# Two first tiles' products inside the routing chain of chunk 0, weight splits spread over its tiles, and the first coefficients loaded tile by tile

## The chip, the cores and the metric

The kernel runs on one core of a Trainium2 chip. The metric is the device time of one execution in microseconds (us); the time of the kernel before is the median of 3 runs. A profile is one execution recorded by the hardware profiler.

## The reference

Two layers run over 8192 tokens of 128 features (32 sequences of 256). Layer 0 adds to x a linear attention and a mixture of 64 experts with one shared expert, both on the normalized rows; layer 1 adds a windowed message network, a sparse top-8 attention and a mixture of 8 experts with 2 chosen. What the change touches is the expert part of layer 0:

```
xn = layernorm(x)
scores = sigmoid(xn @ router_w.T);  sfc = scores + e_bias
keep the 4 best of 8 groups (sum of a group's two largest), then the 8 best experts
coef[t, e] = 2.5 * scores / sum of the chosen, 0 elsewhere
h = silu(xn @ Wg[e]) * (xn @ Wu[e]) * coef[:, e];   out = sum over e of h @ Wd[e]  (+ shared expert)
```

## The kernel before

The tokens go in 16 chunks of 512. Features lie on partitions for the products. In layer 0 two experts of 64 hidden features make one tile of 128, so that a chunk has 33 tiles: 32 of experts and the shared one. All engines follow one plan of steps: step g is tile g of the whole run (chunk g // 33), and each engine does its part of the tile and then the side steps that the tables (`ATTENTION0`, `ROUTE0`, and so on) put at this tile. A list `PROLOGUE` is worked through before step 0.

**A tile.** TensorE (PE) computes at step g the gate and up products of tile g (`first_products`, `mm3`: three products of 128x512, since weights and rows are each split into a high part in a short format and a rest), and then the down product of tile g - 3 (`last_products`, L658). ScalarE (ACT) takes the silu of the gate bank (L1264), VectorE (DVE) multiplies with the up bank (`times_up`, L856) and, one step later, with the tile's coefficients (`times_coef`, L850). There are two gate banks, two up banks, one bank for the down products of a chunk and three side banks for all else. On every engine instructions run in the order written, so a wait holds all that stands behind it. The gate product of tile g waits for the silu of g - 2, the up product for `times_up` of g - 2, and `times_up` of tile g stands on DVE behind `times_coef` of g - 1.

**Coefficients.** DVE computes them for all 64 experts of a chunk in a chain of small operations (steps `sigmoid0` to `weigh`, L887 to L963), PE transposes them (`coefT`, L708), ACT copies them to SBUF (L1334), and the SP queue writes them to DRAM (`keep_coef`, L468). From there SP loads them with a broadcast over 64 partitions: a load (`load_coef`, L477) is two DMAs of 512 KB for the 4 tiles of one place in a ring of 3; a chunk has 8 loads.

**Weights.** In chunk 0 the gate and up weights of every tile are loaded raw by SP (`load_weights`, L417, 128 KB, 10 places) and split: a "split" step is a cast on ACT (L1292) and a subtraction on GpSimd (POOL, L1436), both kept in SBUF. There are 33 such splits, then 16 for the expert weights of layer 1 (L1297, L1439), whose result goes through 2 buffers to DRAM (`w_kept`, L502, 256 KB each): the ACT cast of part k waits until the DMA of part k - 2 has landed. Before, all 33 splits of layer 0 stand in the prologue, 24 of them ahead of the coefficients' transposes, and the 16 others at tiles 1, 3, ..., 31.

**The SP queue** issues all loads in one order. It goes through the splits n = 0, 1, ...: it waits for the POOL part of split n, issues raw weights n + 10, then what `load_rest` puts at n, and for layer 1 the DMA of `w_kept`. The first coefficients stand behind the 24th split, and the second chunk's `keep_coef` behind the last, which is in tile 31.

## Time and profile before

| | |
|---|---|
| median of 3 runs | 1779.98 us (1777.85 to 1780.35) |
| the profiled execution, its own time | 1780.57 us |
| its span | 1778.6 us |
| PE busy | 1713.6 us, 96% of the span |
| DVE, ACT, POOL busy | 1360.6, 806.6, 611.4 us |
| DMA moved | 269.80 MB, 152 GB/s on average |
| PE share of the chain that ended last | 93% |

The page gives busy times per engine and a chain of waits; the trace gives the instructions in order of time (start, duration, engine and line, the idle time before and what ended it), the busy time of each engine in any stretch, and for a DMA the time from issue to landing. Durations of PE are modelled, so the distance between the starts of two products is the better measure. Times below count from the start of the span.

### The profile page before, as it was taken

Reading aid. Unit: us, or ns where it says so; the run is one execution under the profiler, and the core shown is the slowest. Engines: PE = TensorE matmul, PEld = TensorE weight load, DVE = VectorE, ACT = ScalarE, POOL = GpSimd, SP = SyncE. Lnnn points to the kernel's source line nnn. Section 1 sums busy time; section 2 is a strip of 40 time slices with the busy share of each in tenths; the row PEclk is TensorE's granted clock in tenths of the full one; section 3 lists DMA queues with packets and bytes.
Section 4 is the critical chain, followed back from the end, with each engine's and each line's share of the span. In section 5 each row is a group of like instructions: output and inputs, shape, how many; then the busy total and the mean of one; then the engine's idle time right before and its main releaser. Section 6 shows DMA issues by size and latency. Waiting matters only on the chain.

```text
span 1778.6 us, 25081 instructions
## 1 busy us (share of the span) xinstructions
PE 1713.6 (96%) x7292; PEld 1216.1 (68%) x7292; DVE 1360.6 (77%) x4012; ACT 806.6 (45%) x1439; POOL 611.4 (34%) x656
## 2 busy tenths in 40 slices
PE   3999999999999999999999999999999998999995
PEld 2666777777777777777777777777777775667763
DVE  5667879796969797978787887878787877566557
ACT  4435454545444454545454535453545343554431
POOL 6212132323232323232323232232324143467770
PEclk9999999999999999999999999999999999999998
DMA  7948363736373636363736354554545445577759
GB/s 214 257 121 241 88 171 86 177 82 181 78 175 76 179 84 180 82 183 82 181 85 171 94 152 113 136 129 112 151 93 152 105 97 159 178 235 226 266 187 308
DMA packets 166470, 269.80 MB, mean 152 GB/s; under 512 B 13688, under 2 KB 52344, under 8 KB 166080
## 3 DMA queue, kind: packets, MB, share of 16 engines
q1 hardware_dynamic: 157760, 250.50, 52.8%
q0 software_dynamic: 8576, 17.70, 3.1%
q8 instruction: 61, 1.00, 0.2%
q14 instruction: 73, 0.60, 0.1%
HBM read 202.21 MB, written 65.93 MB: 151 GB/s over the span
## 4 chain that ended last, share of the span: by engine, by line
PE 93%; DVE 2%; DMA 1%; POOL 1%; issue 1%; ACT 1%; SPq 0%; DVEq 0%; POOLq 0%; ACTq 0%
PE ps_y L658 25%; PE ps_up L603 8%; PE ps_gate L605 8%; PE ps_up L605 8%; PE ps_gate L603 8%; PE ps_up L604 8%; PE ps_gate L604 8%; PE ps_y L684 4%; PE ps_side L624 3%; PE ps_side L605 2%; PE ps_side L603 2%; PE ps_side L604 2%; PE ps_side L793 1%; PE ps_side L776 1%; PE ps_side L735 1%
## 5 line engine op out<-in xcount | busy, mean ns | idle before, releaser
L856 DVE TENSOR_TENSOR silu_h<-ps_up,silu_h 128x512 f32<-128x512 f32 x618 | 423.6, 685 | 339.7 <-ACT silu_h L1264 271.1
L1264 ACT ACTIVATE silu_h<-ps_gate 128x512 f32<-128x512 f32 x618 | 368.1, 599 | 553.4 <-PE ps_gate L605 551.1
L658 PE MATMUL ps_y<-silu_h,w_dn 128*128 128x512 f32 x1056 | 540.7, 593 | 0.4 <-ACT yT L1270 0.4
L850 DVE TENSOR_TENSOR silu_h<-coef_b,silu_h 128x512 f32<-128x512 f32 x528 | 386.2, 731 | 12.0 <-DMA coef_b<-coef_kept 9.6
L603 PE MATMUL ps_gate<-xnT,w_gu 128*128 128x512 f32 x528 | 318.6, 603 | 0.2 <-ACT silu_h L1264 0.2
L658 PEld LDWEIGHTS ps_y<-silu_h,w_dn 128*128 128x128 f32 x1056 | 199.1, 189 | 54.7 <-issue 7.7
L603 PE MATMUL ps_up<-xnT,w_gu 128*128 128x512 f32 x528 | 209.4, 397 | 13.2 <-DVE silu_h L856 13.2
L605 PE MATMUL ps_gate<-xnT,w_gu 128*128 128x512 f32 x528 | 209.4, 397 | 0.0
L605 PE MATMUL ps_up<-xnT,w_gu 128*128 128x512 f32 x528 | 209.3, 396 | 0.0
L604 PE MATMUL ps_up<-xnT,w_gu 128*128 128x512 f32 x528 | 209.2, 396 | 0.0
L604 PE MATMUL ps_gate<-xnT,w_gu 128*128 128x512 f32 x528 | 208.0, 394 | 0.0
L1514 POOL DMA_INDIRECT slots_x<-rows,slot_of x120 | 133.8, 1115 | 178.2 <-PE ps_gate L605 152.6
L1520 POOL TENSOR_TENSOR msg<-msg 128x512 f32<-128x512 f32 x48 | 65.7, 1368 | 312.3 <-ACT msg L1400 309.8
L1493 POOL DMA_INDIRECT y_kept<-ys,y_to x148 | 145.3, 982 | 59.7 <-issue 38.3
L603 PEld LDWEIGHTS ps_gate<-xnT,w_gu 128*128 128x128 f32 x528 | 100.1, 190 | 60.9 <-issue 56.2
L604 PEld LDWEIGHTS ps_gate<-xnT,w_gu 128*128 128x128 f32 x528 | 100.4, 190 | 60.1 <-issue 55.8
L603 PEld LDWEIGHTS ps_up<-xnT,w_gu 128*128 128x128 f32 x528 | 99.5, 188 | 37.8 <-DVE silu_h L856 15.0
L604 PEld LDWEIGHTS ps_up<-xnT,w_gu 128*128 128x128 f32 x528 | 99.4, 188 | 24.0
L605 PEld LDWEIGHTS ps_up<-xnT,w_gu 128*128 128x128 f32 x528 | 99.4, 188 | 23.7
L605 PEld LDWEIGHTS ps_gate<-xnT,w_gu 128*128 128x128 f32 x528 | 99.5, 188 | 22.9
L1445 POOL TENSOR_TENSOR rstd<-rstd,minus_half 128x4 f32<-128x4 f32 x32 | 43.5, 1360 | 162.2 <-DVE shift L868 162.2
L684 PE MATMUL ps_y<-silu_h,w_down 128*128 128x512 f32 x180 | 91.6, 592 | 0.8 <-DVE silu_h L850 0.8
(266 smaller groups left out, 2699.3 us busy)
## 6 DMA issues: line engine op xcount, KB each, us to landing
coef_b<-coef_kept SPq DMA_DIRECT2D x256, 512.0 KB, 6.7
slots_x<-empty SPq DMA_DIRECT2D x15, 2080.0 KB, 12.2
w_block<-w_kept SPq DMA_DIRECT2D x45, 512.0 KB, 3.9
xs<-slots_x SPq DMA_DIRECT2D x37, 260.0 KB, 3.7
y_back<-y_kept SPq DMA_DIRECT2D x15, 512.0 KB, 6.0
w_raw<-in_ffn_w SPq DMA_DIRECT2D x49, 128.0 KB, 3.9
w_down<-in_ffn_w SPq DMA_DIRECT2D x45, 128.0 KB, 3.7
xres<-in_x SPq DMA_DIRECT2D x16, 256.0 KB, 3.2
```

Source lines behind the costliest of these rows:

```text
L603: eng.matmul(dst, w[0], m[0], start=start, stop=False)
L604: eng.matmul(dst, w[1], m[0], start=False, stop=False)
L605: return eng.matmul(dst, w[0], m[1], start=False, stop=stop)
L624: ins = eng.transpose(ps[:, r * P:(r + 1) * P], rows[:, r * P:(r + 1) * P], ident)
L658: eng.matmul(ps_y[:, :], w_dn[:, j], silu_h[:, g % HBUFS], start=j == 0, stop=last).then_inc(pe_down)
L684: eng.matmul(ps_y[:, :], w_down[:, t % BUFS1, f], silu_h[:, g % HBUFS], start=first, stop=last).then_inc(pe_down)
L850: eng.tensor_tensor(silu_h[:, s], coef_b[:, q % COEF_RING, k], silu_h[:, s], ALU.mult).then_inc(dve_h)
L856: eng.tensor_tensor(silu_h[:, s], ps_up[g % 2][:, :], silu_h[:, s], ALU.mult).then_inc(dve_h1)
L1264: eng.activation(silu_h[:, s], ps_gate[g % 2][:, :], ACT.Silu).then_inc(act_silu)
L1493: eng.indirect_dma_start(y_kept, bass.IndirectOffsetOnAxis(y_to[:, c % XPLACES, r:r + 1], 0), ys[:, c % BUFS1, r], None).then_inc(landed[c ...
L1514: eng.indirect_dma_start(slots_x, bass.IndirectOffsetOnAxis(slot_of[:, r, k:k + 1], 0), rows1[:, c % 2, r], None).then_inc(sent[c % 2], 16)
L1520: eng.tensor_tensor(msg[:, 0], msg[:, 0], msg[:, 1 + k % 2], ALU.add).then_inc(pool_heard)
```

## The change

The prologue keeps 10 splits. The others follow at the end of each tile of chunk 0: one of layer 0 a tile (tile g splits the weights of tile g + 10, up to tile 22), and one of layer 1 in every even tile, the last in tile 30. `SPLIT_ORDER` gives the order in which raw weights are loaded and split. The products, silus and up multiplications of tiles 0 and 1 are steps of the prologue ("gate0", "gate1", "up0", "up1"): the products stand before the transposes of the coefficients, the up multiplications behind them. The key and value products of the first two row blocks move ahead of these transposes as well; `q_sin`, `q_min` and the attention steps move 4 tiles or so back. SP keeps the first coefficients behind the sixth split, and loads the first 4 tiles' coefficients tile by tile (8 DMAs of 128 KB, with semaphores of their own). The constants, the second chunk's rows and the down weights are loaded at earlier places of the SP queue. POOL's fill of the last column of `empty`, which waits for the `common` constants, stands behind the first layer norm's step instead of ahead of it.

```diff
+PROLOGUE = ["stats0", "norm0", "split", "split", "xT0", "split", "x_lo0", "split", "logit0", "split", "score_exp", "split", "gate0", "gate1",
+            "sigmoid0", "sigmoid1", "choice", "pair4", "pair2", "pair1", "gtop", "gstrike", "groups", "top8", "strike", "weigh", "kv0", "kv1",
+            "coefT", "up0", "up1", "kv2", "split", "kv3", "split", "k_rope", "q", "q_cos", "split", "q_swap", "split"]
+TILES_FIRST = 2
+SPLITS_BEFORE = PROLOGUE.count("split")
+SPLITS_BEHIND = [[g + SPLITS_BEFORE] * (g + SPLITS_BEFORE < TILES0) + [TILES0 + g // 2] * (g % 2 == 0 and g < 2 * PARTS1) for g in range(TILES0)]
+SPLIT_ORDER = list(range(SPLITS_BEFORE)) + [part for parts in SPLITS_BEHIND for part in parts]
+EARLY0 = [(1, "q_sin"), (1, "q_min"), (5, "feat_exp"), (7, "q_feat"), (8, "k_feat"), (10, "kvsum"), (11, "kvmask"), (12, "num0"), (13, "num1"), (13, "mix0"),
+          (14, "mix1"), (16, "mixT")]
...
-        if n < SPLITS and g % 2 == 1:
-            plan[g].append(("split", n))
-            n += 1
...
+        if c == 0:
+            plan[g] += [("split", SPLIT_ORDER.index(part)) for part in SPLITS_BEHIND[j]]
...
-                if n == 4:
+                if n == 1:
                     eng.dma_start(c0[:, :], att0_c).then_inc(c0_in, 16)
-                elif n == 12:
+                elif n == 2:
                     load_x(1)
-                elif n in (16, 19, 22):
-                    load_down((n - 16) // 3)
-                elif n == 23:
+                elif n in (3, 4, 12):
+                    load_down((3, 4, 12).index(n))
+                elif n == 15:
                     eng.dma_start(w_out[:, :], att0_f).then_inc(w_out_in, 16)
...
+            def load_coef_tile(k):
+                rows = coef_kept[0].rearrange("(t h) n -> h t n", h=2)
                 for h in range(2):
+                    eng.dma_start(coef_b[h * FF0:(h + 1) * FF0, 0, k], rows[h, k].partition_broadcast(FF0)).then_inc(coef_first[k], 16)
...
+            split_first = [what for what, _ in prologue if what in ("split", "coefT")].index("coefT")
+            loaded = 2
+            for n in range(SPLITS):
+                if n == split_first:
+                    keep_coef(0)
+                    for k in range(COEF_TILES):
+                        load_coef_tile(k)
+                    load_coef(eng, 0, 1)
+                tile = max(g for g, steps in enumerate([prologue] + plan) if ("split", n) in steps) - 1
                 while loaded < COEF_LOADS and tile >= COEF_TILES * (loaded - COEF_RING + 1):
+                    load_coef(eng, 0, loaded)
                     loaded += 1
                 eng.wait_ge(pool_wlo, n + 1)
                 if n + STAGES_W < SPLITS:
                     load_weights(n + STAGES_W)
                 load_rest(n)
...
+            for n, (what, key) in enumerate(prologue):
                 step(what, key)
+                if n == 0:
+                    eng.wait_ge(common_in, 16)
+                    eng.wait_ge(pool_clear, 1)
+                    eng.tensor_scalar(empty[:, :, P + 1], row_of, float(TOP1 * TOKENS), None, ALU.add).then_inc(pool_clear)
```

Three places show the new order. On SP, around the first coefficients, it stood before (n is the split reached):

```order
L417 DMA w_raw<-in_ffn_w 128x256
L455 DMA w_out<-in_att_f 128x128
L468 DMA coef_kept<-coefT 64x512
L477 DMA coef_b<-coef_kept 64x4x512 x2
L417 DMA w_raw<-in_ffn_w 128x256 x9
L477 DMA coef_b<-coef_kept 64x4x512 x4
L417 DMA w_raw<-in_ffn_w 128x256
L502 DMA w_kept<-w_split 128x512
```

and now (L423 is `load_weights`, L474 `keep_coef`, L480 the load by tile, L589 the load of four tiles):

```order
L474 DMA coef_kept<-coefT 64x512
L480 DMA coef_b<-coef_kept 64x512 x8
L589 DMA coef_b<-coef_kept 64x4x512 x2
L423 DMA w_raw<-in_ffn_w 128x256 x4
L589 DMA coef_b<-coef_kept 64x4x512 x2
L423 DMA w_raw<-in_ffn_w 128x256 x2
L502 DMA w_kept<-w_split 128x512
L423 DMA w_raw<-in_ffn_w 128x256
L450 DMA w_dn<-in_ffn_w 128x11x128
L423 DMA w_raw<-in_ffn_w 128x256 x2
L502 DMA w_kept<-w_split 128x512
```

Behind the first coefficients stood 10 raw loads up to the first `w_kept` (34 had gone ahead of them); now 16 have gone ahead, and 6 stand up to the first `w_kept`.

On POOL, from the first layer norm on, it stood before:

```order
L1525 TENSOR_SCALAR empty<-common 128x4
L1445 TENSOR_TENSOR rstd<-rstd,minus_half 128x4
L1447 TENSOR_TENSOR shift<-shift,rstd 128x4
L1436 TENSOR_TENSOR w_gu<-w_raw,w_gu 128x2x128 x29
L1450 TENSOR_TENSOR kf<-kf,tmp 128x512
```

and now:

```order
L1466 TENSOR_TENSOR rstd<-rstd,minus_half 128x4
L1468 TENSOR_TENSOR shift<-shift,rstd 128x4
L1549 TENSOR_SCALAR empty<-common 128x4
L1457 TENSOR_TENSOR w_gu<-w_raw,w_gu 128x2x128 x8
L1471 TENSOR_TENSOR kf<-kf,tmp 128x512
```

29 subtractions stood ahead of the key step, 24 of them ahead of the coefficients' transposes; now 8, and 6 of them ahead of the coefficients.

On ACT, around tiles 4 to 6 of chunk 0, it is now as follows (L1282 is the silu, L1313 and L1318 the casts of the splits of layer 0 and 1, L1362 and L1364 the exponentials of `feat_exp`):

```order
L1313 CAST w_gu<-w_raw 128x2x128
L1318 CAST w_split<-w_raw 128x2x128
L1282 ACTIVATE silu_h<-ps_gate 128x512
L1362 ACT_TABLE_LOAD
L1362 ACTIVATE mix_a<-mix_a 128x512
L1364 ACTIVATE tmp<-tmp 128x512
L1313 CAST w_gu<-w_raw 128x2x128
L1282 ACT_TABLE_LOAD
L1282 ACTIVATE silu_h<-ps_gate 128x512
```

The first silu here is that of tile 5, and the cast ahead of it (L1318) is the third of layer 1, which waits for the first `w_kept`. Before, the third cast of layer 1 stood in tile 5, and `feat_exp` in tile 1.

## Rows read from the trace of the kernel before

**Rows 1.** PE in order of time, first stretch (start us, duration us, idle before)
```profile
32.02 1.06 PE L708 MATMUL ps_side<-common,coef 128*64 128x128 f32 x4 [17.12 <-DVE coef L963]
...
47.78 0.79 PE L603 MATMUL ps_up<-xnT,w_gu 128*128 128x512 f32 x1 [5.47 <-DVE silu_h L856]
```
**Rows 2.** PE in order of time, the end of chunk 0 and the start of chunk 1
```profile
134.53 0.50 PE L603 MATMUL ps_up<-xnT,w_gu 128*128 128x512 f32 x1 [1.67 <-DVE silu_h L856]
...
135.87 1.10 PE L658 MATMUL ps_y<-silu_h,w_dn 128*128 128x512 f32 x2 [0.37 <-ACT yT L1270]
```
**Rows 3.** DVE in order of time, the routing chain of chunk 0
```profile
15.35 0.29 DVE L887 TENSOR_SCALAR score<-score 128x256 f32<-128x256 f32 x1 [3.27 <-ACT score L1329]
...
18.09 0.70 DVE L902 TENSOR_TENSOR struck<-sfc 128x128 f32<-128x128 f32 x1
...
25.65 0.37 DVE L926 MAX8 g_top<-g_a 128x8 f32<-128x8 f32 x4
...
31.54 0.42 DVE L963 SCALAR_TENSOR_TENSOR coef<-struck,wsum 128x256 f32<-128x256 f32 x1
```
**Rows 4.** DVE in order of time, the same operations of chunk 1's routing
```profile
90.00 0.29 DVE L902 TENSOR_TENSOR struck<-sfc 128x128 f32<-128x128 f32 x1
...
90.42 0.69 DVE L850 TENSOR_TENSOR silu_h<-coef_b,silu_h 128x512 f32<-128x512 f32 x1
...
94.06 0.18 DVE L916 TENSOR_TENSOR coef<-coef 128x32 f32<-128x32 f32 x1
...
94.82 0.68 DVE L850 TENSOR_TENSOR silu_h<-coef_b,silu_h 128x512 f32<-128x512 f32 x1
```
**Rows 5.** DVE and POOL in order of time, the first layer norm
```profile
4.88 0.16 DVE L868 TENSOR_SCALAR shift<-mean_var 128x4 f32<-128x4 f32 x1
...
6.50 1.04 POOL L1445 TENSOR_TENSOR rstd<-rstd,minus_half 128x4 f32<-128x4 f32 x1
```
**Rows 6.** SP in order of time, coefficient and kept-weight DMAs
```profile
34.55 0.54 SPq L468 DMA_DIRECT2D coef_kept<-coefT  x1
38.76 1.29 SPq L477 DMA_DIRECT2D coef_b<-coef_kept  x2
...
49.77 0.43 SPq L502 DMA_DIRECT2D w_kept<-w_split  x1
...
121.86 0.50 SPq L468 DMA_DIRECT2D coef_kept<-coefT  x1
```
**Rows 7.** Lines L468 and (second row) L417, the latter up to 40 us, issue to landing
```profile
DMA to landing us min/median/max: 2.3/2.3/4.2
...
DMA to landing us min/median/max: 2.0/3.1/6.8
```
**Rows 8.** ACT in order of time, table load, and the cast behind the first kept weights
```profile
40.63 1.28 ACT L1341 ACT_TABLE_LOAD   x1
...
60.49 0.41 ACT L1297 CAST w_split<-w_raw 128x256 fp32r<-128x256 f32 x1 [4.72 <-DMA w_kept<-w_split]
```
**Rows 9.** Busy time by stretch (engines, PEclk, DMA share, GB/s last)
```profile
40.00:70.00 30.00, 24.53 (x100) 17.29 (x101) 18.20 (x38) 13.18 (x25) 12.19 (x14) 0.89 1.06 265
...
50.00:60.00 10.00, 10.00 (x40) 6.92 (x39) 5.41 (x8) 2.62 (x6) 2.41 (x2) 0.89 1.07 243
60.00:70.00 10.00, 10.00 (x50) 7.37 (x49) 6.74 (x14) 3.52 (x8) 1.86 (x3) 1.00 1.06 294
...
54.00:56.00 2.00, 2.00 (x11) 1.54 (x10) 1.26 (x3) 1.19 (x2) 0.00 (x0) 1.00 1.07 218
```
**Rows 10.** PE in order of time, chunk 0: kvsum, and the gates of tiles 8 and 27
```profile
58.72 1.05 PE L727 MATMUL ps_side<-v,kf 128*128 128x129 f32 x8
...
61.54 0.72 PE L603 MATMUL ps_gate<-xnT,w_gu 128*128 128x512 f32 x1
...
107.16 0.80 PE L603 MATMUL ps_gate<-xnT,w_gu 128*128 128x512 f32 x1
```
**Rows 11.** Line L850 from 48 to 110 us (min/median/max ns)
```profile
L850 DVE TENSOR_TENSOR silu_h<-coef_b,silu_h x26: 627/684/1253, 47.8 to 109.2; 128x512 f32<-128x512 f32 x26
```

More of the change, by code:

```diff
@@ L320, in build_program @@
         coef_out, coef_in = sem("coef_out"), [sem(f"coef_in{n}") for n in range(COEF_RING)]
+        coef_first = [sem(f"coef_first{n}") for n in range(COEF_TILES)]
         act_whi, pool_wlo = sem("act_whi"), sem("pool_wlo")
@@ L522, in sync @@
                 keep_coef(c)
-                load_coef(c, 0)
+                load_coef(eng, c, 0)
                 if c >= 2:
@@ L579, in sync, with load_coef @@
             eng.wait_ge(stored, 16 * CHUNKS)
+        def load_coef(eng, c, k):
+            q = c * COEF_LOADS + k
+            if q >= COEF_RING:
+                eng.wait_ge(dve_h, COEF_TILES * (q - COEF_RING + 1))
+            rows = coef_kept[c].rearrange("(t h) n -> h t n", h=2)
+            for h in range(2):
+                eng.dma_start(coef_b[h * FF0:(h + 1) * FF0, q % COEF_RING],
+                              rows[h, k * COEF_TILES:(k + 1) * COEF_TILES].partition_broadcast(FF0)).then_inc(coef_in[q % COEF_RING], 16)
         def load_rows(eng, t):
@@ L686, in step @@
             def step(what, key):
+                if what in ("gate0", "gate1"):
+                    first_products(int(what[4]))
                 if what in TAKES:
@@ L1286, in step @@
                 c = key
-                if what == "split":
+                if what in ("gate0", "gate1"):
+                    silu(int(what[4]))
+                elif what == "split":
                     n = key
@@ L1290, in step @@
                     eng.wait_ge(w_in[n % STAGES_W], 16 * (n // STAGES_W + 1))
-                    if n < TILES0:
-                        eng.copy(w_gu[:, n, :, 0], raw).then_inc(act_whi)
+                    part = SPLIT_ORDER[n]
+                    if part < TILES0:
+                        eng.copy(w_gu[:, part, :, 0], raw).then_inc(act_whi)
                     else:
-                        k = n - TILES0
+                        k = part - TILES0
                         if k >= 2:
@@ L1522, in gpsimd @@
             eng.memset(empty[:, :, :], 0.0).then_inc(pool_clear)
-            eng.wait_ge(common_in, 16)
-            eng.wait_ge(pool_clear, 1)
-            eng.tensor_scalar(empty[:, :, P + 1], row_of, float(TOP1 * TOKENS), None, ALU.add).then_inc(pool_clear)
-            for what, key in prologue:
+            for n, (what, key) in enumerate(prologue):
                 step(what, key)
+                if n == 0:
+                    eng.wait_ge(common_in, 16)
+                    eng.wait_ge(pool_clear, 1)
+                    eng.tensor_scalar(empty[:, :, P + 1], row_of, float(TOP1 * TOKENS), None, ALU.add).then_inc(pool_clear)
             for g in range(STEPS):
```

61 lines of the change are left out of this document (22 added, 39 removed).

## The prediction

> **What bounds the kernel now.** The page comes first: PE is busy for 96% of the span and carries 93% of the chain that ended last, so time can only be won where PE stands still or runs slowly. The idle time in PE's timeline then says where: 17.12 us ahead of the transposes of the first coefficients (32.02) and 5.47 us ahead of the up product at 47.78, which follows the first coefficients' landing [rows 1]; 1.67 and 0.37 us at the border of chunk 1 [rows 2]. Behind that PE is full to the last stage. So the case is decided in the first 135 us, and the views to read are the timelines of each engine there, and the DMA rate by stretch [rows 9], since all waits of this stage end in DMAs.
>
> **The coefficient path.** Four parts of it get shorter.
> - The first layer norm: DVE is done at 5.04, POOL takes up rstd at 6.50 [rows 5], since its fill of `empty` waits for constants. The fill now stands behind: 1.4 us earlier for all that follows.
> - The routing chain on DVE runs from 15.35 to 31.96 [rows 3], 16.6 us. The eleven operations from L902 to the start of L926 take 7.56 us. In chunk 1 the same take 0.42 us for the first two and 0.76 for the last five [rows 4], so about 2.0 for eleven. What differs is POOL: beside the chain of chunk 0 it worked off 19 splits. Those are gone from there (front: 6 instead of 24 ahead of the coefficients). 5.6 us saved here, and about 0.9 on the two operations behind L933, which are of the same kind: 6.5. The chain ends at 31.96 - 1.4 - 6.5 = 24.0.
> - From there to the write to DRAM it took 2.6 us (34.55 [rows 6]), partly because SP stood in weight loads; now ACT has two copies of values ahead of the coefficients' copy, which wait for 1.2 us of DVE. I take 2.2: the write goes out at 26.2.
> - It landed 4.2 us later [rows 6] in a busy queue; the median is 2.3 [rows 7], and the queue will be empty: 28.5. A tile's coefficients are then two issues of 0.64 us (1.29 for two, [rows 6]) and a landing as that of other 128 KB loads, 2.0 to 3.1 us [rows 7]: they are there at about 32, where PE waited until 47.78, hence some 14 us earlier. Tiles 0 to 3 have their first products by then (before: 3 and a half tiles), which is worth half a tile and is left at nothing.
>
> This would be the gain if coefficients were all that chunk 0 needs. They are not.
>
> **The DMA queue.** Splits moved out of the prologue take their loads with them. Counted from the order on SP: until the coefficients are kept, only 5.3 MB are asked for (16 raw weights, constants, rows, two of three parts of the down weights), and from about 18 to 28.5 us the queue carries nothing. Chunk 0 needs 24.2 MB in all (49 raw weights of 0.131 MB, 16 kept parts of 0.262, 8 coefficient loads of 1.05, the rest 5). So 18.9 MB are left behind 28.5, where before 13 MB were left at 47.8.
>
> What waits for them is ACT. Its cast of layer 1's part k waits for the landing of part k - 2, and the silus of all later tiles stand behind it. In the trace of before this wait is there: the write issued at 49.77 lets ACT go at 60.49 [rows 6, 8], 10.7 us later, though PE did not feel it. Now the third such cast stands in tile 4 instead of 5, and `feat_exp`, with a table load of 1.28 us [rows 8] and another for the way back, directly behind it in tile 5, where it once lay in the wait for the first coefficients.
> - First kept part: the 8 small loads are through at about 34.7. Up to this part stand 3.15 MB (loads 1 and 2, six raw weights, the part). At 265 GB/s, the rate of 40 to 70 us where the queue was full [rows 9], that is 11.9 us. In before, 4.7 MB were asked from 38.76 up to the first part; at 265 GB/s and 2 us of latency it would have landed at 58.5, and it landed some 2 us behind that, so 34.7 + 11.9 + 2 = 48.6.
> - Then ACT: cast 0.4, silu of tile 5 0.6, table 1.28, two exponentials 1.2, cast 0.4, table 1.28, silu of tile 6 0.6 = 5.8. The gate of tile 8 waits for this: 54.4. Before it started at 61.54 [rows 10]. **7.1 us earlier.**
> - From there PE needs what it needed before, 107.16 - 61.54 = 45.6 us for 19 tiles [rows 10], and the `kvsum` products, which now lie behind, 1.05 at most and 0.8 by the spacing of starts: gate of tile 27 at 100.8.
> - The queue sets a second bound for the same tile. From the first kept part to the eleventh, which frees the cast in tile 24, I count 13.4 MB: 50.7 us at 265 GB/s, 99.3, and 1.1 us for cast and silu: 100.4. The two bounds meet. Gain at tile 27: 107.2 - 100.8 = **6.4 us**.
>
> Behind tile 27 only five kept parts are left, so the queue has air.
>
> **The border of chunk 1.** `keep_coef` of chunk 1 went out at 121.86 [rows 6], behind the split of tile 31. The last split is in tile 30 now, and a tile takes 45.6 / 19 = 2.4 us with its side work. That is more than the 1.67 PE waited, and the 0.37 (ACT was held by values that DVE had not reached) goes with it [rows 2]: **2.0 us**. Next in line there is nothing late.
>
> **Costed at nothing.** The numbers of products, silus and multiplications are the same. The silus of tiles 0 and 1 and their table load lie under the routing chain (10 us). Six more DMA issues for the small loads are in the 34.7 above. PE is cold where it starts again at 24: in rows 1 to 10 it had the same restart with a lower granted clock (0.89 mean from 40 to 70 us [rows 9]); a restart behind the wait for the kept part is hidden by the 5.8 us of ACT. The later q steps are due by tile 16 and lie beside PE. If this cover goes, a second cold restart costs about 2 us.
>
> **The sum.** 6.4 + 2.0 = 8.4 us against the profiled execution's 1780.57: 1772.2. The median of the runs is 0.6 lower, so the forecast is **1771.6**.
>
> **A rule against the change.** The eight small loads are priced above by rows of 128 KB. The Trainium skill, "DMA: Bandwidth & Descriptors", section Bandwidth, wants DMAs of 1 MiB or more and gives 138 GB/s for 64 KB; by that figure the 1.05 MB would take 7.6 us, an estimate from that page, 2.6 more than the issues need, and the forecast would be 1774.2. The trace has 128 KB loads landing in 2.0 to 3.1 us, several under way at once, and I hold to that.
>
> **Rivals.**
> 1. *The kept parts don't hold ACT.* If the queue moved the 60 to 70 us rate, 294 GB/s [rows 9], all along, the eleventh part would land at 34.7 + 56.3 + 2 = 93.0, tile 27 could start at 94.1, and the gain is 13 + 2: 1765. For: that row. Against: it is the best 10 us of a full queue. 0.17.
> 2. *The queue is a little slower*, 240 to 250 GB/s: at 245 the eleventh part lands at 104.4, tile 27 at 105.5, gain 1.7 + 2: 1776. For: from 50 to 60 us it was 243 [rows 9]. 0.16.
> 3. *Slower than before.* Same mechanism, place and price: with coefficient loads, raw weights and kept parts mixed, the rate was 218 GB/s at a share of 1.07 [rows 9]. At 220 the eleventh part lands at 112.1, tile 27 starts at 113.2, 6 us behind before, less 2 of the border: 1784. It decides below 232 GB/s, where 34.7 + 16.6 MB + 2 + 1.1 passes 109.2. Against: no row of 10 us is as slow. 0.07.
> 4. *DVE becomes the bound.* 23 splits more lie beside the coefficient products on DVE, which took 684 ns as median and 1253 at worst [rows 11]. One collision of 0.57 a tile over the 15 tiles with such a split would be 8.5 us, of which DVE's free time (18.20 of 30 us busy, rows 9) takes most; where routing fills DVE, five tiles, 1.5 to 3 us come through: 1774. The Trainium skill, "SBUF - State Buffer", section Who interferes with whom, states the lock: an operation of DVE with two SBUF inputs and one of GpSimd that reads SBUF exclude each other for a whole instruction. 0.08.
> 5. *It does nothing measurable*: rate near 235, or a wait that I don't see behind the table loads. 0.04.
>
> **Chances.** Forecast 0.48. A difference of over 0.2% (3.6 us) is about what a measurement of this kernel can tell. Faster by that: the forecast, rivals 1 and 4, and three quarters of 2: 0.85; within: the rest of 2 and rival 5, 0.08; slower: rival 3, 0.07. The range leaves out rival 3 and the ends of 1: 1764.5 to 1778.5.
>
> **What would show it.** Right: coefT's transposes near 24 us, the first coefficient product near 32, a DMA share near 0 from 18 to 28 us and about 1 from 30 to 100; an idle time of ACT ahead of a layer-1 cast that ends near 49; the gate of tile 8 near 54, that of tile 27 near 101; no PE wait near 125. Wrong: PE full from 33 us on (rival 1), the same ACT waits at all casts up to tile 24 with PE waiting each time (2, 3), or waits for DVE while ACT has none (4).

## The result, and the profile after

| | before | changed |
|---|---|---|
| median of 7 runs each | 1779.44 us (1777.85 to 1780.35) | 1773.12 us (1772.39 to 1774.14) |
| profiled execution, own time | 1780.57 us | 1772.39 us |
| its span | 1778.6 us | 1770.4 us |
| PE busy | 1713.6 us | 1714.8 us |

The ratio is 0.9966, 95% interval 0.9955 to 0.9978: faster by 6.3 us, where 8.4 were forecast. The interval allows 4 to 8 us. PE works as long as before; the lead over the kernel before is 4.24 us at tile 27 and 6.8 us behind the border of chunk 1, and it is still 6.8 us at the first tile of the last chunk (1399.35 against 1406.15 us).

PE of the changed kernel in order of time, chunk 0: the coefficients' transposes, and the gates of tiles 7, 8 and 27. These answer to [rows 1, 10].
```profile
24.71 1.03 PE L721 MATMUL ps_side<-common,coef 128*64 128x128 f32 x4 [5.10 <-DVE coef L981]
...
52.12 0.76 PE L614 MATMUL ps_gate<-xnT,w_gu 128*128 128x512 f32 x1 [8.75 <-ACT silu_h L1282]
...
56.79 0.47 PE L614 MATMUL ps_gate<-xnT,w_gu 128*128 128x512 f32 x1 [0.34 <-ACT silu_h L1282]
...
102.92 0.80 PE L614 MATMUL ps_gate<-xnT,w_gu 128*128 128x512 f32 x1
```
The wait of 17.12 us for the coefficients is down to 5.10, that of 5.47 us is gone, and a new one of 8.75 has come at tile 7 (52.12), for a silu of ACT. From tile 8 on PE doesn't wait in chunk 0. Tile 8 comes 4.75 us earlier than before, tile 27 4.24 earlier.

DVE, the chain of chunk 0's routing and the first coefficient product; answers to [rows 3].
```profile
14.32 0.29 DVE L905 TENSOR_SCALAR score<-score 128x256 f32<-128x256 f32 x1 [3.28 <-ACT score L1350]
...
16.98 0.29 DVE L920 TENSOR_TENSOR struck<-sfc 128x128 f32<-128x128 f32 x1
...
19.19 0.37 DVE L944 MAX8 g_top<-g_a 128x8 f32<-128x8 f32 x4
...
24.14 0.42 DVE L981 SCALAR_TENSOR_TENSOR coef<-struck,wsum 128x256 f32<-128x256 f32 x1
...
32.32 0.69 DVE L866 TENSOR_TENSOR silu_h<-coef_b,silu_h 128x512 f32<-128x512 f32 x1 [1.72 <-DMA coef_b<-coef_kept]
```
The chain took 10.2 us (14.32 to 24.56) where it took 16.6, and its eleven operations from L920 on 2.2 us instead of 7.56.

SP in order of time: the write of the coefficients, their loads by tile, the second and third load (L589), the first part for layer 1, and chunk 1's write; answers to [rows 6]. Below it line L502, issue to landing; then ACT's first cast that waits for a part, answering to [rows 8].
```profile
26.39 0.53 SPq L474 DMA_DIRECT2D coef_kept<-coefT  x1
28.70 4.94 SPq L480 DMA_DIRECT2D coef_b<-coef_kept  x8
33.69 1.29 SPq L589 DMA_DIRECT2D coef_b<-coef_kept  x2
35.02 2.78 SPq L423 DMA_DIRECT2D w_raw<-in_ffn_w  x4
37.84 1.25 SPq L589 DMA_DIRECT2D coef_b<-coef_kept  x2
39.13 1.07 SPq L423 DMA_DIRECT2D w_raw<-in_ffn_w  x2
40.24 0.43 SPq L502 DMA_DIRECT2D w_kept<-w_split  x1
...
115.36 0.50 SPq L474 DMA_DIRECT2D coef_kept<-coefT  x1
```
```profile
DMA to landing us min/median/max: 2.0/4.8/10.8
```
```profile
51.08 0.40 ACT L1318 CAST w_split<-w_raw 128x256 fp32r<-128x256 f32 x1 [7.12 <-DMA w_kept<-w_split]
51.39 0.59 ACT L1282 ACTIVATE silu_h<-ps_gate 128x512 f32<-128x512 f32 x1
```
The part is written at 40.24 and has landed 10.8 us later, at 51.08. Until then the cast that reuses its buffer stands at the head of ACT's queue, the silu behind it starts at 51.39, and PE's gate behind that at 52.12.

Busy time by stretch in the changed kernel (columns as in rows 9: PE, PEld, DVE, ACT, POOL, PEclk, DMA share, GB/s).
```profile
20.00:28.00 8.00, 3.29 (x13) 2.96 (x14) 7.31 (x40) 1.94 (x7) 0.18 (x1) 0.62 0.22 55
...
28.00:34.70 6.70, 5.69 (x21) 3.75 (x20) 4.57 (x15) 2.35 (x7) 6.70 (x7) 0.95 0.47 144
34.70:40.20 5.50, 4.20 (x17) 2.57 (x17) 2.46 (x5) 4.00 (x10) 5.33 (x7) 1.00 0.91 224
40.20:51.10 10.90, 3.17 (x11) 1.60 (x9) 1.03 (x2) 0.43 (x2) 3.13 (x5) 0.76 1.10 259
...
80.00:100.00 20.00, 20.00 (x76) 13.52 (x75) 17.72 (x49) 9.33 (x22) 8.48 (x12) 1.00 0.96 264
```
The DMA engines are nearly idle from 20 to 28 us, then filling, and full or nearly so from 40 us on. A share a little over 1 is read as full here.

### The profile page after: what moved, and what is told of

The parts are those of the page before. It is cut to its first block, busy times and chain, and to the rows that moved or that the text cites. A ratio compares the mean times of both kernels' runs of the same rounds, so it can differ in the third digit from the quotient of the medians.

```text
span 1770.4 us, 25093 instructions
## 1 busy us (share of the span) xinstructions
PE 1714.8 (97%) x7292; PEld 1216.5 (69%) x7292; DVE 1355.2 (77%) x4012; ACT 805.9 (46%) x1439; POOL 615.0 (35%) x656
## 4 chain that ended last, share of the span: by engine, by line
PE 93%; DVE 3%; ACT 1%; DMA 1%; POOL 1%; issue 1%; SPq 0%; DVEq 0%; POOLq 0%; ACTq 0%
PE ps_y L669 25%; PE ps_gate L616 8%; PE ps_up L616 8%; PE ps_up L614 8%; PE ps_gate L614 8%; PE ps_up L615 8%; PE ps_gate L615 8%; PE ps_y L695 4%; PE ps_side L635 3%; PE ps_side L616 2%; PE ps_side L614 2%; PE ps_side L615 2%; PE ps_side L806 1%; PE ps_side L789 1%; PE ps_side L748 1%
## 5 line engine op out<-in xcount | busy, mean ns | idle before, releaser
L1282 ACT ACTIVATE silu_h<-ps_gate 128x512 f32<-128x512 f32 x618 | 368.3, 599 | 545.7 <-PE ps_gate L616 543.0
L866 DVE TENSOR_TENSOR silu_h<-coef_b,silu_h 128x512 f32<-128x512 f32 x528 | 387.8, 735 | 7.9 <-DMA coef_b<-coef_kept 5.4
```

The source lines that it names most:

```text
L866: eng.tensor_tensor(silu_h[:, s], coef_b[:, q % COEF_RING, k], silu_h[:, s], ALU.mult).then_inc(dve_h)
L1282: eng.activation(silu_h[:, s], ps_gate[g % 2][:, :], ACT.Silu).then_inc(act_silu)
```

## The experiments

A "part" is one of the 16 pieces of layer 1's weights that chunk 0 splits and writes to DRAM. **Theory A**: what decides is how long the write of a part takes to land in the full queue. With two buffers the cast of part k waits at the head of ACT's queue for the landing of part k - 2, and silus, DVE and PE stand behind it. **Rival C**: the bytes themselves are the bound at some 260 GB/s, so that whatever is won early comes back as another wait. **Third**: the start (early products, loads by tile, splits outside the routing chain) decides. The expectations of runs 1 to 3 use other letters: what is Rival C here is Theory B there, and Theory C of run 1 is that the table loads of `feat_exp` set tile 8.

Read side by side, for the profiled execution of each kernel: when PE starts the gates of tiles 8 and 27 in chunk 0 and of tile 38, behind the border of chunk 1. Where each profile's first row transposes start varies by 0.7 us (8.37 to 9.09 in the changed kernel and its variants, 9.64 to 9.86 in before and its two), so that much of a row's place is not the edit's. The numbers are those of the sections below.

| kernel | tile 8 | tile 27 | tile 38 | time as ratio to before |
|---|---|---|---|---|
| before | 61.54 | 107.16 | 140.20 | 1 |
| changed | 56.79 | 102.92 | 133.43 | 0.9966 (0.9955 to 0.9978) |
| 1. second load later | 50.52 | 101.94 | 132.45 | 0.9957 (0.9941 to 0.9973) |
| 2. parts from tile 6 | 46.16 | 104.34 | 135.50 | 0.9973 (0.9960 to 0.9985) |
| 3. the same, late loads early | 46.39 | 100.99 | 131.49 | 0.9950 (0.9934 to 0.9967) |
| 4. late loads early only | 56.26 | 102.90 | 133.40 | 0.9964 (0.9951 to 0.9978) |
| 5. four buffers | 49.83 | 98.56 | 129.06 | 0.9933 (0.9920 to 0.9947) |
| 6. four buffers, parts from tile 6, loads early | 45.92 | 92.49 | 122.99 | 0.9914 (0.9898 to 0.9929) |
| 7. four buffers, loads early | 50.45 | 96.58 | 127.09 | 0.9951 (0.9932 to 0.9971) |
| 8. gates behind the routing | 58.03 | 104.15 | 134.66 | a single run |
| 9. first coefficients in one load | 55.64 | 106.62 | 137.13 | 0.9960 (0.9941 to 0.9979) |
| 10. four splits in the routing chain | 55.89 | 102.02 | 132.53 | a single run |
| 11. before, parts at even tiles | 65.71 | 111.46 | 141.96 | 1.0005 (0.9995 to 1.0014) |
| 12. the same as 11, four buffers | 62.50 | 108.06 | 138.57 | 0.9987 (0.9971 to 1.0003) |

Runs 7, 9, 10 and 12 fell on a chip on which before took 1828.19 us. The stages up to tile 38 read as on the others, but from 1200 to 1750 us the granted clock was 0.97 in all four, against 1.00 in the changed kernel on its chip. Their times are compared by ratio alone.

**1. The second coefficient load behind the first part.**
```diff
-                while loaded < COEF_LOADS and tile >= COEF_TILES * (loaded - COEF_RING + 1):
+                while loaded < COEF_LOADS and tile >= COEF_TILES * (loaded - COEF_RING + 1) + 2 * (loaded == 2):
```


> Changed kernel, with the third load of coefficients (1.05 MB, first needed at tile 8) issued behind the first kept part instead of ahead of it. Theory A (PE waits at tile 7 because the first kept part stands behind 3.15 MB in the queue): the cast that waited until 51.1 us goes about 4 us earlier, near 47, and the gate of tile 8 with it, from 56.8 to about 53. Theory B (the queue's capacity sets the end of chunk 0): the casts of tiles 22 and 24 keep their times (94.1 and 99.4 us), so the gate of tile 27 moves from 102.9 to about 100.5 and no further, and the whole kernel gains 2.4 us on the changed one; by A alone it would be 4. Theory C (the table loads of feat_exp set tile 8): no change.

ACT's wait ends at 44.81 instead of 51.08 us, and PE comes to tile 8 6.3 us earlier. At tile 27 1.0 us of it is left.
```profile
44.81 0.41 ACT L1318 CAST w_split<-w_raw 128x256 fp32r<-128x256 f32 x1 [2.02 <-DMA w_kept<-w_split]
```
```profile
55.81 0.47 PE L614 MATMUL ps_gate<-xnT,w_gu 128*128 128x512 f32 x1 [1.55 <-ACT silu_h L1282]
```
The landing of the first part sets tile 8, as A has it, and what stands ahead of the part in the queue sets the landing: 6.9 us behind the write (37.92 to 44.81) instead of 10.8. That tile 8 moved with no change to `feat_exp` rules out the table loads as what alone sets it; they are 2.6 us of the work that ACT does behind the landing, and no run moved them. The first landing does not set the end: later parts' landings take their turn (ACT waits of 4.02 us at 54.69 and 4.69 at 61.97). Of the 5.3 us that are lost again between tiles 8 and 27, 3.1 are idle time of PE (1.55 us ahead of tile 9, 1.56 at 69.32), and in the rest PE runs slowly (granted clock 0.72 from 56 to 58 us and 0.50 from 58 to 60). Neither forecast was met: both gains at the first cast and at tile 8 were larger than A's (47 and 53 us expected), and the casts of tiles 22 and 24, which were to keep their times by Theory B, came 1.7 and 0.7 us later. The median, 1772.89 us, can't be told from the change's 1773.12.

**2. Parts for layer 1 from tile 6 on**, at tiles 6, 8, ..., 22, 23, ..., 29.
```diff
-SPLITS_BEHIND = [[g + SPLITS_BEFORE] * (g + SPLITS_BEFORE < TILES0) + [TILES0 + g // 2] * (g % 2 == 0 and g < 2 * PARTS1) for g in range(TILES0)]
+PARTS_AT = list(range(6, 23, 2)) + list(range(23, 30))
+SPLITS_BEHIND = [[g + SPLITS_BEFORE] * (g + SPLITS_BEFORE < TILES0) + [TILES0 + k for k, at in enumerate(PARTS_AT) if at == g] for g in range(TILES0)]
```


> Changed kernel, with the 16 splits of layer 1 at tiles 6, 8, ..., 22 and then 23 to 29, so that none stands in the first six tiles. Theory A: the 8.8 us wait of PE ahead of tile 7 goes; the gate of tile 8 comes near 46 instead of 56.8. Theory B: later casts wait for the queue instead; part 6 is asked for behind about 14.7 MB and lands near 87, so the gate of tile 27 comes at 93 to 96 instead of 102.9, and the kernel gains 7 to 9 us on the changed one (1764 to 1766). If waits for weights were not what holds PE, nothing moves.

**3. The same, and the late loads asked early**: the last down weights, `w_out`, `raw1`, `f1`, `b1`, `causal` and x of chunks 2 and 3 at n == 5 in `load_rest`, while the queue is nearly idle.
```diff
-                elif n in (3, 4, 12):
-                    load_down((3, 4, 12).index(n))
...
+                elif n == 5:
+                    load_down(2)
+                    eng.dma_start(w_out[:, :], att0_f).then_inc(w_out_in, 16)
+                    eng.dma_start(raw1[:, :], att1_w).then_inc(raw1_in, 16)
...
+                    load_x(3)
```


> As the run with the parts from tile 6, and in addition the last down weights, the output weights, the constants of layer 1 and the rows of chunks 2 and 3 (2.0 MB) are asked for at the sixth split, in the stretch of 20 to 28 us where the queue carried 55 GB/s. Theory B: these 2.0 MB are 7.7 us of queue at 265 GB/s that are gone from the full stretch, so the queue no longer sets the end and the gate of tile 27 comes near 91 (PE alone): about 12 us on the changed kernel, near 1761. If capacity does not matter once the order is right, it equals the run before it.

Both come to tile 8 at 46 us, as expected, and then lose most of it in one place. ACT, DVE and PE of the third run, in order of time:
```profile
62.64 0.40 ACT L1317 CAST w_split<-w_raw 128x256 fp32r<-128x256 f32 x1 [6.46 <-DMA w_kept<-w_split]
63.06 1.28 ACT L1281 ACT_TABLE_LOAD   x1
64.35 0.60 ACT L1281 ACTIVATE silu_h<-ps_gate 128x512 f32<-128x512 f32 x1
```
```profile
64.98 0.69 DVE L871 TENSOR_TENSOR silu_h<-ps_up,silu_h 128x512 f32<-128x512 f32 x1 [9.27 <-ACT silu_h L1281]
65.59 0.41 DVE L1012 TENSOR_TENSOR kv<-ps_side,att_const 128x256 f32<-128x256 f32 x1
```
```profile
66.39 1.30 PE L747 MATMUL ps_side<-kv,qf 128*128 128x144 f32 x4 [5.95 <-issue]
```
PE's wait is marked "issue", for which no releaser is shown. The other two engines tell it: the products of L747 need `kv`, which DVE writes at 65.59, behind a multiplication that waited 9.27 us for a silu, which stood on ACT behind a cast that waited for a part's landing. It is the same wait of the third part's cast as at 51 us in the changed kernel, moved from tile 4 to tile 10. Moving parts moves this wait; it does not remove it. Run 2 had 7.12 us of PE at the same place. Both forecasts for the end failed, and clearly: run 2 was to reach tile 27 at 93 to 96 us and 1764 to 1766 us, and came at 104.34 with a median of 1775.90; run 3 was to reach it near 91 with 1761 us, and came at 100.99 with 1771.26. They had the first casts right and left out that the third part's cast would wait in its turn. What the two runs leave open is why the landing costs anything: A or C.

**4. The late loads early, nothing else** (the diff of run 3 on the changed kernel).

> The changed kernel with the late loads (the last down weights, w_out, layer 1's raw1, f1, b1, causal, and x of chunks 2 and 3: about 2.0 MB) asked in the idle stretch of the queue ahead of 28 us, the parts as in the changed kernel. Rival C: 2.0 MB less behind 30 us is worth 2.0 MB / 260 GB/s = 7.7 us of queue by tile 27, but PE waits only where a load is late, so the first cast's wait (7.12 us) shrinks by what of these bytes was ahead of it, the last down weights for the most part (704 KB, 2.7 us); median 1769 to 1771 us. Theory A (landing alone, whatever the bytes): the wait at 51 us stays within 1 us of 7.12, median 1772 to 1774 us.

```profile
50.55 0.40 ACT L1316 CAST w_split<-w_raw 128x256 fp32r<-128x256 f32 x1 [7.21 <-DMA w_kept<-w_split]
```
The loads did go out early: from 20 to 28 us the queue moved 310 GB/s instead of 55, that is 2.0 MB more. The wait is 7.21 us instead of 7.12, tile 27 starts at 102.90 instead of 102.92, and the median is 1772.99, in the range that A gave. At the first wait this is a weak test, since none of these bytes had been asked for ahead of the first part (the last down weights went out at 41.19 us in the changed kernel, the part at 40.24); the expectation had that order wrong, and run 1 is the one that moved bytes there. For the rest of chunk 0 it is a strong one: the waits of ACT for later parts fell from 5.8 us to 0.8 in all between 55 and 105 us, and PE came to tile 27 no earlier. Some 2.0 MB less behind 28 us changed nothing for PE: against C as the first bound.

**5. Four buffers for the parts.** The two more lie in `xnT1`, which is not used before layer 1. The lines left out give each buffer a semaphore of its own and let all later waits count four.
```diff
+        def split_of(k):
+            if k % 4 < 2:
+                return w_split[:, k % 4]
+            return xnT1[:, k % 4 - 2].rearrange("p (a b d) -> p a b d", a=2, b=2)
...
-                        if k >= 2:
-                            eng.wait_ge(w_kept_out[k % 2], 16 * (k // 2))
-                        eng.copy(w_split[:, k % 2, :, 0], raw).then_inc(act_whi)
+                        if k >= 4:
+                            eng.wait_ge(w_kept_out[k % 4], 16 * (k // 4))
+                        eng.copy(split_of(k)[:, :, 0], raw).then_inc(act_whi)
```


> The changed kernel with four buffers for the parts that are split for layer 1 instead of two (the two more lie in xnT1, which nothing uses before layer 1); the order of the work is the same. Theory A (the landing of a part's write holds the next cast by the two-buffer ring, and through ACT's queue the silus and PE): the cast that waits 7.12 us at 51.08 us waits nothing, PE comes to tile 8 at 56.79 - 8.75 - 0.34 = 47.7 us, the other waits of ACT for w_kept are gone too, PE comes to tile 27 at 102.92 - 9.1 = 93.8 us and the median is 1764 to 1766 us. Rival C (the bytes behind each other in the full queue are the bound, at about 260 GB/s): the same bytes are asked in the same order, so what is won at tile 8 comes back as a wait for a coefficient load, for w_raw or for the fifth part's buffer between 55 and 75 us; tile 27 stays between 100 and 103 us and the median between 1770.5 and 1773.

**6. Four buffers with the order of run 3.**

> The kernel of the run that splits layer 1's parts from tile 6 on and asks the last loads early, with four buffers for the parts. There a cast at 62.64 us had waited 6.46 us for a buffer, and PE 5.95 us behind it at 66.39 us. Theory A: that wait is gone, PE comes to tile 27 at 100.99 - 5.95 = 95.0 us, median 1765 to 1766 us. Rival C: another wait of 3 to 6 us takes its place (for w_raw or a coefficient load), tile 27 at 98 to 101 us, median 1769 to 1772 us.

ACT and PE of run 5, in order of time, then PE and a stretch of run 6:
```profile
43.35 0.41 ACT L1319 CAST w_gu<-w_raw 128x256 fp32r<-128x256 f32 x1 [3.40 <-DMA w_raw<-in_ffn_w]
...
54.54 0.41 ACT L1324 CAST w_split<-w_raw 128x256 fp32r<-128x256 f32 x1 [1.43 <-DMA w_raw<-in_ffn_w]
```
```profile
45.16 0.47 PE L620 MATMUL ps_gate<-xnT,w_gu 128*128 128x512 f32 x1 [1.59 <-ACT silu_h L1288]
...
49.83 0.47 PE L620 MATMUL ps_gate<-xnT,w_gu 128*128 128x512 f32 x1 [2.19 <-ACT silu_h L1288]
...
98.56 0.80 PE L620 MATMUL ps_gate<-xnT,w_gu 128*128 128x512 f32 x1
```
```profile
44.66 0.50 PE L619 MATMUL ps_up<-xnT,w_gu 128*128 128x512 f32 x1 [1.25 <-DVE silu_h L877]
...
92.49 0.80 PE L619 MATMUL ps_gate<-xnT,w_gu 128*128 128x512 f32 x1
```
```profile
34.00:60.00 26.00, 24.66 (x99) 16.49 (x100) 18.65 (x28) 19.35 (x38) 18.22 (x21) 1.00 1.04 243
```
In run 5 no cast waits for a part any more, PE waits 3.8 us at tiles 7 and 8 instead of 9.1, and the median is 1768.38 (before, on the same chip: 1780.45). In place of these waits stand shorter ones for raw weights, and tile 27 is at 98.56. That is between the forecasts, 93.8 of A and 100 to 103 of C, and so is the median (1764 to 1766 and 1770.5 to 1773). Of the 4.8 us that A's forecast was short, 2.1 are lost by tile 8, 1.6 between tiles 8 and 9, where PE runs without a wait at a lower granted clock (0.57 from 50 to 54 us), and 1.0 at tile 12. In run 6 ACT's longest wait for a raw weight behind 50 us is 2.28 us and PE does not feel it, tile 27 is at 92.49, and the median is **1764.27** (1762.47 to 1766.13), the best kernel here and below A's forecast of 1765 to 1766. So A is the first bound, shown by taking away what makes the cast wait. Behind it stands a second one of some 6 us at tile 27 (98.56 to 92.49): waits for raw weights and the slow products behind them, which the order of parts and loads takes away.

**7. Four buffers, loads early, the parts where the change has them.**

> The changed kernel with four buffers for the parts and the late loads asked early; the parts for layer 1 in the tiles of the changed kernel. With four buffers ACT waited for raw weights instead (43.35 us, 3.40; 54.54, 1.43; 62.16, 1.24), and PE some 5 us in all. If these waits are the queue's bytes (theory C, second in line): 2.0 MB less behind 30 us takes most of them, tile 27 from 98.56 to 95 or 96 us, median 1765 to 1766 us. If the place of the parts is what gave the rest in the run with parts later: median 1767.5 to 1769 us.

```profile
43.98 0.41 ACT L1317 CAST w_gu<-w_raw 128x256 fp32r<-128x256 f32 x1 [4.82 <-DMA w_raw<-in_ffn_w]
```
Tile 27 is at 96.58, 2.0 us before run 5 and just outside the 95 to 96 that were expected from the bytes. But the trace does not bear out the bytes as the cause: ACT's wait for a raw weight at 44 us is longer than in run 5 (4.82 instead of 3.40 us), and tile 8 comes 0.6 us later, at 50.45. All of the gain lies behind tile 8, and 1.6 us of it between tiles 8 and 9, where run 5 ran at the lower clock:
```profile
50.00:54.00 4.00, 4.00 (x11) 2.49 (x10) 3.73 (x5) 2.51 (x6) 3.48 (x4) 0.57 1.13 341
```
Run 7 has a granted clock of 1.00 there. The step to run 6 is another 4.1 us, and tile 8 comes 4.5 us earlier in it. So what takes the second bound away is the place of the parts; that the early loads help is not shown. The time does not resolve this: the interval holds ratios from 0.9932 to 0.9971.

**8. The products gate0 and gate1 behind coefT.**
```diff
-PROLOGUE = ["stats0", "norm0", "split", "split", "xT0", "split", "x_lo0", "split", "logit0", "split", "score_exp", "split", "gate0", "gate1",
+PROLOGUE = ["stats0", "norm0", "split", "split", "xT0", "split", "x_lo0", "split", "logit0", "split", "score_exp", "split",
...
-            "coefT", "up0", "up1", "kv2", "split", "kv3", "split", "k_rope", "q", "q_cos", "split", "q_swap", "split"]
+            "coefT", "gate0", "gate1", "up0", "up1", "kv2", "split", "kv3", "split", "k_rope", "q", "q_cos", "split", "q_swap", "split"]
```


> The changed kernel with the products gate0 and gate1 of the first tiles moved from inside the routing chain to behind coefT. Theory A: they are no term of the time, since PE waits for the coefficients behind them: routing chain on DVE 24.56 +- 0.3 us at its end, first coefficient product at 32.3 +- 0.4, tile 8 at 56.8 +- 0.7 us, time within 1 us of 1772.4. Rival (the early products are what lets PE and ACT start on the tiles): gate0 to the first coefficient product moves 1 us or more later, tile 8 too, time 1773.5 us or more.

PE starts gate0 at 25.61 instead of 13.68, the first coefficient product runs at 35.47 instead of 32.32, and PE comes to tiles 8, 27 and 38 1.2 us later, of which 0.2 is the profile's later start. The cast behind the first part's landing goes at 52.32 instead of 51.08. A's forecast was wrong here: with the first tiles late, all that stands behind them on ACT is late, the first part's write too (42.24 us instead of 40.24). The early products are worth about 1.0 us in this profile; the own time, 1773.71, is a single run and settles nothing.

**9. The first coefficients in one load.**
```diff
-                    for k in range(COEF_TILES):
-                        load_coef_tile(k)
+                    load_coef(eng, 0, 0)
...
```


> The changed kernel with the first four tiles' coefficients asked as one load (two DMAs of 512 KB) instead of eight of 128 KB. Theory A (the first casts for layer 1 decide, not the first coefficients): the first coefficient product moves from 32.3 to about 35 us (1.05 MB at 260 GB/s and 2 us of landing behind 28.7), SP has 6 issues less and is free 3 to 4 us sooner; PE comes to tile 8 at 55 to 58 us, median within 1.5 us of 1773.1. Rival (loads by tile are a term of their own): what the first product loses, 2.7 us, is lost at tile 8 and at the end, median 1775 us or more.

DVE, then two stretches of this run:
```profile
37.14 0.69 DVE L862 TENSOR_TENSOR silu_h<-coef_b,silu_h 128x512 f32<-128x512 f32 x1 [6.04 <-DMA coef_b<-coef_kept]
```
```profile
58.00:62.00 4.00, 4.00 (x16) 3.30 (x15) 3.86 (x4) 0.60 (x2) 4.00 (x4) 0.50 1.01 316
62.00:66.00 4.00, 4.00 (x9) 2.48 (x8) 1.39 (x2) 0.89 (x2) 1.18 (x2) 0.50 0.95 231
```
The first product comes 4.8 us later than in the changed kernel (2.7 were expected), and yet PE is at tile 8 1.15 us earlier, since SP is free earlier: the part goes out at 37.20 and has landed at 49.93. As A had it, the first coefficients don't set tile 8. But tile 27 is 3.7 us later: PE was idle 2.20 and 2.18 us ahead of tiles 7 and 8, and from 58 to 66 us its granted clock is 0.50, that is 1.2 GHz, so that from tile 8 to tile 11 it took 13.85 us instead of 8.99, without a wait. The ratio, 0.9960, can't be told from the change's 0.9966. Whether loads by tile are worth anything stays open.

**10. Four splits in the routing chain**, between `choice` and the step behind `pair1`, instead of behind `kv2`.
```diff
-            "sigmoid0", "sigmoid1", "choice", "pair4", "pair2", "pair1", "gtop", "gstrike", "groups", "top8", "strike", "weigh", "kv0", "kv1",
-            "coefT", "up0", "up1", "kv2", "split", "kv3", "split", "k_rope", "q", "q_cos", "split", "q_swap", "split"]
+            "sigmoid0", "sigmoid1", "choice", "split", "pair4", "split", "pair2", "split", "pair1", "split", "gtop", "gstrike", "groups", "top8", "strike", "weigh", "kv0", "kv1",
+            "coefT", "up0", "up1", "kv2", "kv3", "k_rope", "q", "q_cos", "q_swap"]
```


> The changed kernel with four of its splits (POOL subtraction 0.73 us, ACT cast 0.40 us each) moved from behind the coefficients into the routing chain, between choice and pair1. If POOL beside the chain is what made it slow in the kernel before (19 splits, 5.4 us on the eleven small operations): DVE's chain ends 1.1 to 2.2 us later than 24.56, the write of coefT too. If it was not: the chain ends at 24.6 +- 0.3. On the time, Theory A: the loads of four raw weights (0.5 MB, 2 us) leave the full queue, against a start that is 1 to 2 us later: within 1.5 us of 1772.4.

```profile
14.75 0.29 DVE L905 TENSOR_SCALAR score<-score 128x256 f32<-128x256 f32 x1 [3.28 <-ACT score L1350]
...
18.95 0.72 DVE L936 TENSOR_TENSOR coef<-coef 128x32 f32<-128x32 f32 x1
19.70 0.65 DVE L938 TENSOR_TENSOR coef<-coef 128x32 f32<-128x32 f32 x1
20.39 0.65 DVE L940 TENSOR_TENSOR g_a<-g_a,coef 128x32 f32<-128x32 f32 x1
...
26.06 0.42 DVE L981 SCALAR_TENSOR_TENSOR coef<-struck,wsum 128x256 f32<-128x256 f32 x1
```
From the start of its first to the start of its last operation DVE's chain takes 11.31 us here and 9.82 in the changed kernel: 1.5 us more, inside the expected 1.1 to 2.2. POOL's four subtractions run from 18.83 to 21.67 us, and three operations of DVE in that stretch make up all of the 1.5: they take 0.72, 0.65 and 0.65 us instead of 0.18, 0.19 and 0.19. In before, beside 19 subtractions, each of the eleven took 0.61 to 0.81. So POOL beside the chain is what had slowed it; ACT's four casts, which moved too, were over at 19.67. By the rule that the prediction cited from the Trainium skill, "SBUF — State Buffer", section Who interferes with whom, an operation of DVE with two SBUF inputs and one of GpSimd that reads SBUF exclude each other. The trace agrees: the three long ones are such operations, and each takes about as long as one subtraction (0.73 us), while the MAX8 behind them, with one input, keeps its 0.37 us beside the last subtraction. Tile 38 comes 0.9 us earlier all the same.

**11. Before, with the parts at even tiles** (the last one at tile 30), **and 12. with four buffers as well.** Run 11 is this edit, run 12 adds the one of run 5.
```diff
-        if n < SPLITS and g % 2 == 1:
+        if n < SPLITS and g % 2 == 0:
...
-                tile = 2 * k + 1
+                tile = 2 * k
```


> The kernel before, with one part of the change alone: the splits of layer 1 at even tiles (0 to 30) instead of odd ones (1 to 31), everything else as before. The theory on the border of chunk 1 (the second chunk's coefficients stand on SP behind the last split) expects that the waits of 1.67 and 0.37 us there go and that all later chunks lead by 2 to 2.5 us: 1777 to 1777.5. Rival: these waits are for the rate of the queue and not its order: no change.

And of run 12:

> The kernel before with layer 1's parts at the even tiles (last one at tile 30, as in the change) and four buffers for them; nothing else of the change. With two buffers the earlier parts gave 2.5 us at the border of chunk 1 and lost as much in the first tiles (ACT waited 7.96 us for a part's landing at 60.84 us, PE 2.60 us behind it). Theory A: with four buffers that loss is gone and the border's gain stays, tile 27 at 107 us, median 1777 to 1778 us. Rival: the loss comes from the queue's bytes, median 1779.5 to 1781 us.

ACT and PE of run 11:
```profile
60.84 0.40 ACT L1297 CAST w_split<-w_raw 128x256 fp32r<-128x256 f32 x1 [7.96 <-DMA w_kept<-w_split]
```
```profile
62.37 0.49 PE L603 MATMUL ps_gate<-xnT,w_gu 128*128 128x512 f32 x1 [2.60 <-ACT silu_h L1264]
```
From tile 27 to tile 38 run 11 gains 2.54 us on before and run 12 2.53, as the change does (2.53): the border's gain comes from the earlier last part alone. But run 11 is 4.30 us late at tile 27, since one tile earlier is enough to turn the landing, which PE did not feel before, into a wait of 2.60 us. With four buffers that wait is gone and the loss at tile 27 is 0.90. The time of run 11, 1780.81 us, missed the 1777 to 1777.5 that were expected: the gain at the border came, and the loss ahead of it, which was not foreseen, ate it up. Run 12 lies where Theory A put it (0.9983 to 0.9989 as a ratio), but 0.9987 with an interval up to 1.0003 shows no gain and does not exclude the rival.

## Why the prediction was right, and where it was off

The measured median, 1773.12 us, lies 1.5 above the forecast and within the range, and the mechanism is the one forecast: the coefficients come early, ACT waits for the landing of the first part, and that sets tile 8. One term of the sum was mis-sized, the landing; a smaller one, the border, came out larger than said and hid 0.5 us of it.

- **Layer norm, 1.4 us.** The transposes of the rows start at 8.61 instead of 9.64, the chain 1.03 earlier: a little over-priced, by less than the 0.7 us by which profiles differ here.
- **Routing chain, end at 24.0.** 24.56. The eleven operations took 2.2 us (2.0 forecast), and run 10 shows their cause.
- **The write at 26.2, landed at 28.5, first product at about 32.** 26.39, 28.70 (2.3 us), 32.32. The eight loads were issued in 4.94 us, each landed 2.9 to 3.3 us behind its issue, and 3.6 us behind the first issue their first product ran. Run 9, with DMAs of 512 KB, had its first product at 37.14.
- **The rule held against the change.** The Trainium skill, "DMA: Bandwidth & Descriptors", section Bandwidth, gives 64 KB DMAs 138 GB/s; the 7.6 us for the whole megabyte are an estimate from that. The trace does not contradict it: the last of the eight was issued at 33.0 us and landed 2.9 to 3.3 us later, at most 7.6 us behind 28.70. But no more than two of the eight stand ahead of the first product, so the 2.6 us that this rule would have added did not come up there.
- **The part's landing at 48.6: this is the term that was mis-sized.** It was 51.08. I took 265 GB/s from 34.7 us on. From 34.7 to 40.2 it was 224 GB/s, at a share of 0.91, probably because SP did not fill the queue faster: 1.0 us of this stretch it waited for POOL's splits. No run tested that. These 5.5 us at 224 and the rest of the 3.15 MB at 259 put it at 47.6, 1.0 us behind the 46.6 of my sum without latency; the other 1.5 us lie behind that, a landing 3.5 us behind its bytes where I took 2. The prediction had the sign of this in its own rows: in before the same formula gave 58.5 where the cast went at 60.49, and the 2 us by which it fell short were not carried over. With them the landing would have been forecast at 50.6. Why it falls short stays open; the stretches from 28 to 51.1 us moved some 5.0 MB, 0.8 more than was asked for up to and with the part, so by this estimate some of what was issued behind the part moved ahead of its last byte.
- **ACT's 5.8 us behind it.** 5.71 (51.08 to 56.79). So tile 8 came at 56.8 and not 54.4, and the gain there was 4.75 and not 7.1.
- **19 tiles in 46.4 us.** 46.13. Thus tile 27 at 102.9, and 4.24 us instead of 6.4; that one landing, 2.5 us late, is more than the whole difference of 2.1.
- **The second bound, eleventh part at 99.3.** The cast stood until 99.43, so the place was forecast well, but it was no bound for tile 27: in run 4 the same cast went at 97.99 without a wait, and tile 27 started at 102.90 all the same. Nor did the bytes hold PE: with four buffers tile 27 started at 98.56, 96.58 and 92.49. That "the two bounds meet" was therefore wrong. The prediction had named the wait, "part k waits for the landing of part k - 2", and never asked what a third buffer would do.
- **The border, 2.0 us.** 2.53, and the same in runs 11 and 12.
- **At nothing.** The gates of tiles 0 and 1 are worth about 1.0 us and not nothing (run 8). The cold restart behind the wait for the part was hidden, as said: the granted clock was 0.50 from 46 to 56 us and 0.99 from 56 to 58, and tile 8, at 56.79, still had to wait 0.34 us for ACT's silu.
- **The queue from 18 to 28 us.** It was said to carry nothing; it moved 104 GB/s there on average, and 55 from 20 us on.
- **The sum** in the profile: 4.24 + 2.53 = 6.77, which is the lead at tile 38 and matches the 6.3 of the medians. The own times differ by 8.18; the 1.4 more come behind the start of the last chunk (1399 us), where nothing was changed, and no run says why.
- **Rivals.** Rival 1 (queue at 294 GB/s, tile 27 at 94) did not come; rivals 2 and 3 needed under 250 and 232 GB/s, and it was 259 in the stretch that counts. Rival 4: L866 took 686 ns as median and 1731 at worst from 48 to 110 us, against 684 and 1253 [rows 11], without a wait of PE for it.

## What to carry to other kernels

Where a buffer is reused after a DMA's landing and the queue is full, count buffers by the landing time (10.8 us here, over four tiles of work at 2.4 us) and not by how often the buffer is needed; an in-order engine at the head of such a ring passes the wait to everybody. A load moved out of a prologue has to land in the stretch behind it: ask first which ring it will make wait. When a change has taken a 17 us stall away and little comes of it, look for the first long wait on the engine that stands between, and test it by more buffers before the order is tuned. Check the granted clock before a difference of 1 or 2 us is put down to bytes.

## What the runs showed that was not expected

- The landing time of a 256 KB write goes from 2.0 to 10.8 us in the same queue of the changed kernel. With 1.05 MB less ahead of it the first part's fell from 10.8 to 6.9 us (run 1).
- After the stalls of these runs PE often came back at the lower of its two clocks, and how much this cost differs. In run 2 PE idled 7.12 us ahead of 67.34; from 66 to 70 us the granted clock was 0.50 and from 70 to 74 0.56:
```profile
66.00:70.00 4.00, 2.66 (x8) 2.40 (x9) 3.96 (x8) 0.98 (x3) 1.49 (x2) 0.50 1.09 266
70.00:74.00 4.00, 4.00 (x11) 2.64 (x11) 2.86 (x7) 1.20 (x3) 1.46 (x2) 0.56 1.07 279
```
  Tiles 12 to 16 took 20.28 us there and 9.98 in the changed kernel: 7.1 of idle time and 3.2 at 1.2 GHz. In run 9 two idle times of 2.2 us, far shorter, were followed by a granted clock of 0.50 in every microsecond from 57 to 67 us while PE was busy, and tiles 8 to 11 took 4.9 us longer. In run 6, with no idle time over 1.25 us there, the clock was 1.00 from 34 to 60 us.
- Four POOL subtractions of 0.73 us beside a chain of small DVE operations lengthened three of these from 0.2 us to 0.65 to 0.72, about the length of one subtraction each, and the chain by 1.5 us (run 10).
